# Moving the query projection in TensorE's order of the second attention

## The reference

```python
q = (x @ w_q).reshape(bsz, q_len, H, HD).transpose(0, 2, 1, 3)      # H = 32, HD = 128
lq = x @ w_lq
lk = (lq @ w_lk)...;  lv = (x @ w_lv)...                             # 32 latent heads
q = _apply_rope(q, cos, sin); k = ...; lk = _apply_rope(lk, cos, sin)
attn = _causal_attn(q, k, v, SCALE)                                  # 8 key heads, each for 4 query heads
lat = _causal_attn(q, lk, lv, SCALE)
return attn @ w_o + lat @ w_lo
```

## Time and profile before

| what | value |
|---|---|
| median of 3 runs | 2422.95 us (2421.2 to 2423.99) |
| the profiled execution | 2422.93 us, its span 2421.1 us |
| TensorE matmul / weight load busy | 93% / 82% of the span |
| VectorE busy | 75% |
| GpSimd busy | 65% |
| ScalarE busy | 59% |
| the second attention | about 783 to 2193 us of the span |

### The profile page before, as it was taken

How to read it: one execution, slowest core, us unless ns; L and a number is a source line. 1 busy time by engine, 2 the same in 40 slices (tenths; PEclk the granted TensorE clock), 3 DMA queues, 4 the chain that set the end, 5 groups by cost and what they waited for, 6 DMA issues and landing times. The chain is left out here.

```text
span 2421.1 us, 43785 instructions
## 1 busy us (share of the span) xinstructions
PE 2239.8 (93%) x14144; PEld 1987.9 (82%) x14144; DVE 1804.6 (75%) x3266; ACT 1433.2 (59%) x3949; POOL 1577.2 (65%) x1340
## 2 busy tenths in 40 slices
PE   6899999988999899999999999999999999987998
PEld 5788888876888788888888888888888888876886
DVE  5788777767633898888888888888888888964332
ACT  2657766653233676676666666676676766663232
POOL 3656657413364678878878878788788788642343
PEclk8999999988999999999999999999999999988999
DMA  3201111000000101101101111111111111004000
GB/s 102 63 24 46 58 34 44 11 2 26 19 25 25 47 15 56 55 20 55 48 26 58 39 39 50 39 45 43 40 46 47 31 50 41 19 5 148 1 18 18
DMA packets 49556, 95.39 MB, mean 39 GB/s; under 512 B 6768, under 2 KB 14224, under 8 KB 48976
## 3 DMA queue, kind: packets, MB, share of 16 engines
q1 hardware_dynamic: 49296, 92.24, 12.2%
HBM read 81.47 MB, written 10.75 MB: 38 GB/s over the span
## 5 line engine op out<-in xcount | busy, mean ns | idle before, releaser
L1290 POOL TENSOR_TENSOR a_nf_acc<-a_nf_acc,a_nf_term 128x512 f32<-128x512 f32 (+1 forms) x416 | 588.9, 1416 | 145.4 <-ACT a_nf_term L1390 76.7
L1348 ACT ACTIVATE a_probs<-bank,q_packed 128x128 f32<-128x128 f32 (+1 forms) x512 | 208.4, 419 | 193.4 <-DVE q_packed L1640 193.4
L1357 ACT ACTIVATE a_probs<-a_probs,q_packed 128x128 f32<-128x128 f32 (+1 forms) x512 | 192.5, 463 | 68.9 <-DVE q_packed L1646 68.9
L1848 POOL TENSOR_TENSOR f_w_lo<-WGU,f_w_hi 128x512 fp32r<-128x512 f32 x88 | 112.4, 1295 | 175.5 <-ACT f_w_hi L1891 175.5
L1271 POOL TENSOR_TENSOR a_qk_lo<-q_packed,a_qk_hi 128x512 fp32r<-128x512 f32 (+1 forms) x160 | 193.7, 1212 | 44.5 <-ACT a_qk_hi L1334 44.5
L64 PE MATMUL bank<-a_wo_hi,a_ot_hi 128*128 128x512 f32 x512 | 212.5, 415 | 0.0
L1651 DVE TENSOR_TENSOR e_pt_lo<-bank,q_hot 128x384 fp32r<-128x384 f32 x256 | 141.0, 551 | 91.2 <-ACT q_hot L1367 90.4
L1710 DVE TENSOR_SCALAR a_nf_term<-a_nf_unit 128x512 f32<-128x512 f32 (+1 forms) x288 | 200.1, 740 | 3.4 <-DVE a_nf_unit L1693 0.9
L66 PE MATMUL bank<-a_wo_hi,a_ot_lo 128*128 128x512 f32 x512 | 201.4, 393 | 0.0
L65 PE MATMUL bank<-a_wo_lo,a_ot_hi 128*128 128x512 f32 x512 | 201.1, 393 | 0.0
L1334 ACT ACTIVATE a_qk_hi<-q_packed 128x512 fp32r<-128x512 f32 (+1 forms) x160 | 94.3, 590 | 176.0 <-DVE q_packed L1625 176.0
(11 more groups left out here) (244 smaller groups left out, 8461.1 us busy)
## 6 DMA issues: line engine op xcount, KB each, us to landing
q_packed<-in_l_o SPq DMA_DIRECT2D x64, 256.0 KB, 2.8
q_packed<-in_l_vk SPq DMA_DIRECT2D x32, 384.0 KB, 3.1
q_packed<-in_l_ql SPq DMA_DIRECT2D x32, 320.0 KB, 2.9
a_raw<-in_l_ou SPq DMA_DIRECT2D x32, 288.0 KB, 2.8
a_raw<-in_l_nr SPq DMA_DIRECT2D x16, 384.0 KB, 3.0
a_nf_raw<-in_w_nf SPq DMA_DIRECT2D x24, 256.0 KB, 2.6
coded_w<-a_nf_acc SPq DMA_DIRECT2D x24, 256.0 KB, 2.0
f_codes<-coded_w SPq DMA_DIRECT2D x6, 512.0 KB, 3.8
```

The source lines that it names most:

```text
L1290: pool.tensor_tensor(acc, left, nf_term[:, i % CODE_RING, 0:w], ALU.add).then_inc(nf_added, 1)
L1348: act.activation(probs[:, n % 2, col:col + keys], bank[:, at:at + keys], ACT.Exp, bias=dip[:, n % 2, i:i + 1], accum_out=total[:, n % 2, i ...
L1357: ins = act.activation(cell, cell, ACT.Copy, scale=share[:, n % 2, i:i + 1])
L1848: pool.tensor_tensor(lo, src, hi.bitcast(F32), ALU.subtract).then_inc(part_lo[i], 1)
```

## The change

In each step of the second attention, TensorE's `project` of the query unit (always the first of the step's units) moves from directly behind `scores(n)` to behind `turn(n - 1, 0)`, directly ahead of `output(n - 3)`. Nothing is added or removed, no wait value changes, and the other engines keep their order.

```diff
                 for n in range(STEPS):
                     scores(n)
                     units = l1_step_units(n, last)
-                    for name in units[0:1]:
-                        project(name)
                     if not (first and n < 2):
                         apply(n - 2)
                     if not (first and n < 1):
                         turn(n - 1, 0)
+                    for name in units[0:1]:
+                        project(name)
                     if not (first and n < 3):
                         output(n - 3)
                     if not (first and n < 1):
```

## The result

The changed kernel takes **2411.97 us** (median; 2409.82 to 2412.84), the kernel before, measured beside it, 2422.07 us (2421.1 to 2423.99). The ratio is 0.9957, 95% interval 0.9946 to 0.9967: 10.1 us less, where the forecast was 3.2 less.

A forecast was written before the change was run, and what follows sets the result against it. The DVE-ACT chain was taken to set the end, with TensorE having some slack. Per group -0.74 + 0.29 = -0.45 us, over seven groups -3.2 us, gave 2422.9 - 3.2 = 2419.7 us; range 2414 to 2431 us.

The forecast's parts named there:

- No direct relief: Second transposes (L1519, 56.5 us of waits): they come earlier only if the DVE-ACT chain does, so no gain was given.
- Rival F: Second transposes wait less because a product fills the time: at most 56.5 us, near 2370 us; chance 0.04.
- Step 9's stall: TensorE stands about 1.07 us at apply; about 0.29 us per group reaches the chain at step 11's scores.
- Steps 13 and 14: TensorE stands 2.0 us at step 13's apply; step 14's scores come 1.73 us late, hidden by less than 0.1 us.
- rival E: TensorE at 1.2 GHz after new waits of steps 9 and 13: +12 us, 2435 us; chance 0.07.
- The flip: Step 12: L1625 of DVE starts 0.16 us ahead of POOL's L1290, takes 0.69 us and saves 1.17 more.
- Kept of it: Of the chain's 1.44 us lead in step 13, 0.74 us per group stays after the next L1625 meets POOL's L1262.
- First and last group: Last group given nothing: POOL further ahead in step 12, no query product following in steps 14 and 15; seven groups counted.
- rival C: L1625 wins in step 13 too, the chain keeps 1.44 us per group: 8.1 us less, 2414.8 us; chance 0.13.
- B: Order with POOL at step 12's L1625 does not turn round, step 11's 0.29 us remain: 2424.9 us; chance 0.24.
- D: L1625 loses a turn at POOL's port elsewhere, 1.17 us per group: +8.2 us, 2431.1 us; chance 0.10.
- G: The order is of no consequence in any of these places: 2422.9 us; chance 0.04.

The follow-up runs named there:

- the kernel without the stalling steps: The changed kernel with the old order kept in steps 5, 7, 8, 9, 13 and 14, where TensorE would stand longest at apply: 2411.38 us.
- the pad of 256 columns: The changed kernel with one more DVE reduction of 256 columns, result unused, in step 12 of each group: 2422.93 us.

## Why the prediction was wrong in size, point by point

**What bounds the kernel: right.** TensorE's waits went up by 11.6 us and the time down by 10; the kernel without the stalling steps moved 20 us of waits between two lines at the same time. The chain through DVE and ACT sets the end. The evidence that I gave for it was weaker than it looked: the 172.6 and 173.4 us of the earlier trace rows come from stretches cut at other edges. Counted from peaks to peaks the two groups take 173.37 and 172.94, the one with half clock in it the longer by 0.4; other groups of the loop at full clock take 173.2 and 173.4. The experiments carry the claim, not those two numbers.

**No direct relief: right.** L1519's waits fell by 13 us, to 43.4, while L64's rose by 25, to 33.1; the forecast was about 40, and 35 to 55. Rival F is out.

**Step 9's stall: a term that didn't arrive.** I charged 0.29 us per group. PE in steps 9 to 11 of the fourth group, to be held against the earlier trace rows (the changed kernel is 4.32 us ahead there):

```profile
1401.83 0.39 PE L64 MATMUL bank<-q_hot,a_vl_hi 128*128 128x256 f32 x1 [0.89 <-DVE e_pt_lo L1651]
...
1419.25 0.39 PE L64 MATMUL bank<-q_hot,XT_hi 128*128 128x320 f32 x1
...
1421.09 0.34 PE L64 MATMUL bank<-q_hot,XT_hi 128*128 128x320 f32 x1
...
1422.88 0.28 PE L64 MATMUL bank<-a_qk_hi 128*128 128x256 f32 x1
```

The stall is there (0.89 us of idle time, second transposes 1.17 us late; I had 1.07 and 1.17). The first side unit of step 10 is 1419.25 + 4.32 - 1423.03 = 0.54 late, the second 0.08, the scores of step 11 0.01. I had carried 0.83 through step 10 and taken off only the wait that the second unit's row shows; the wait ahead of the second transposes of step 10 (some 0.15 us) and the slower first matmuls behind each wait (0.41 against 0.34 us) go too when a stall has come before. A delay of TensorE that passes two waits is swallowed by both. That is 7 x 0.29 = 2.0 us too many.

**Steps 13 and 14: right.** The stall fell to 0.29 us since the chain is early, and the chain kept its time there. The price of rival E shows in the kernels without the flip: 1.5 us at step 13 in a group that meets the half clock, against the 1.7 that the rival had; it came in four groups of eight and five of eight, not in all.

**The flip: right in mechanism and place.** L1625 of step 12 went from 1.86 to 0.69 us in seven groups, and POOL's operation beside it was stretched. ACT's out_high came 0.38 us earlier against 0.27 forecast, the peaks of step 13 came 1.54 early against 1.44.

**Kept of it: mis-sized.** I kept 0.74 us; 1.04 stayed (1.54, less 0.50 at L1625 of step 13, where I had 0.70). POOL's L1290, stretched, took 1.73 us; by the lead of 0.16 us in the prediction it would have had to wait 0.53 us and take 1.96, a step that the prediction used and did not write down. And POOL lost the 1.29 us in which it stood before L1271. Its L1262 in step 13 came 1.02 us earlier, not 0.76, and let DVE through sooner. That is 7 x 0.3 = 2.1 us too few.

**First and last group: the step that failed outright.** "I give it nothing" was a guess on the last group. ACT waits for apply there in three steps, and each is on the chain: 0.44 us gained at step 11, 0.38 at step 12, 0.5 at step 14, in all 1.35 us without any flip. (In step 14 ACT had waited only 0.23 us, and a stretch of 6.8 us at half clock in that step is gone too; the kernel that keeps the old order in steps 12 and 13 keeps both and gains only the first of the three. The share of each in the 0.5 is open.) The first group has 0.4 us of the same kind in step 3. The rows for it (L1373's waits for L66, 21 of them in the kernel before, 2 after) I had read for one group of the loop alone. These are 1.7 us. With the tail counted the last group gained 1.76 us.

**The sum, corrected:** 7 x 1.04 + 1.35 + 0.4 = 9.0 us, of 9.4 in the block and 10.1 in all. The rest, some 1 us, is not explained: in the profiled executions 0.4 stand in the tail, 0.4 ahead of the block, and 0.4 in the block's groups. The forecast had 3.2; the missing 5.8 are 2.0 + 2.1 + 1.7. The number came out near rival C (8.1 us less), but its condition, POOL no earlier in step 13, did not hold. B, D and G are out.

**The range** reached to rival C and no further, and rival C charged the 0.29 us of step 11 too: without that it ends at 2412.8, still 0.8 above what was measured. A term that I charged to every case should have stood at zero in one of them, and no case allowed for a gain in the first and the last group.

## What to carry to other kernels

Where two engines share a port, ask of each change which of their meetings it turns round: the sign of a few tenths of a microsecond at one step decided 10 us here, and the same work moved in the other steps of the middle groups decided next to nothing. A gain at such a meeting must be followed along both queues until they meet again, since the engine that lost the turn is late for everything behind it, sums that the winner waits for included. Waits of the busiest engine are no gain to be had where another chain sets the pace, and a part of a block written out apart (a first, a last group) needs a reading of its own.

## What of the hardware I had not expected

- The loss of a turn at the port has a sharp edge: 0.69 us at a lead of 0.13 us, 1.83 and more at a lag of 0.08 to 0.12, for the same add of 128x512. Behind the edge it shrinks as DVE comes later (1.68 us at 0.30, 1.35 at 0.62). The operation that had to give way to it grew by only 0.30 to 0.42 us (L1290 at 1.73 and 1.83 against 1.41 to 1.43).
- TensorE's granted clock fell to 1.2 GHz for some 3.4 us behind a wait of 1.85 us, in a loop in which it is 94% busy, and in the same step of group after group (step 13 of four with all but step 12 moved, of five with the pad of 256 columns; step 14 of five with neither 12 nor 13 moved). At step 0 of the changed kernel's groups three waits (2.02, 2.08 and 2.55 us) passed without it, while one of 2.04 and one of 2.59 were followed by 3.4 us at half clock. Why this step so often isn't settled.
